# Layer 0 of a four-layer conditioned network: the quantised values are transposed by a DMA, the down projection stands at the step's end, and the y path runs one tile later

## The reference, cut to what matters

```python
def act_quant(x):
    scale = 127.0 / jnp.clip(jnp.max(jnp.abs(x), axis=-1, keepdims=True), 1e-05, None)
    return jnp.clip(jnp.round(x * scale), -128.0, 127.0) / scale
scale = cond @ norm_w.T + 1.0
ms = jnp.mean(x * x, axis=-1, keepdims=True)
h = x * (scale[:, None, :] * jax.lax.rsqrt(ms + EPS))
u = h @ up_w.T                                  # 256 -> 2 x 1024
val, gate = jnp.split(u, 2, axis=-1)
h = val * jax.nn.gelu(gate, approximate=False)
hq = h + jax.lax.stop_gradient(act_quant(h) - h)      # whole numbers -127..127, per token
wq = down_w + jax.lax.stop_gradient(weight_quant(down_w) - down_w)   # -1, 0, 1 times a scale
y = hq @ wq.T                                   # 1024 -> 256
return y + x
```

## Time and profile before

| | |
|---|---|
| median of 3 runs | 845.87 us (844.93 to 846.77) |
| profiled execution | 844.1 us, its span 842.3 us |
| granted clock | 0.99 over the span |
| PE busy | 807.0 us, 96% of the span |
| DVE, POOL, ACT busy | 65%, 49%, 48% |

### The profile page before, as it was taken

One profiled execution on the slowest core, in us unless ns is written; L12 is line 12 of the kernel. 1 busy time (PEld: TensorE's weight loads), 2 busy tenths in 40 slices (PEclk: granted clock), 3 DMA queues, 4 the chain that ended last, 5 costly groups with the idle time before them and its releaser, 6 DMA issues.

```text
span 842.3 us, 20010 instructions
## 1 busy us (share of the span) xinstructions
PE 807.0 (96%) x7116; PEld 645.7 (77%) x7116; DVE 543.9 (65%) x933; ACT 405.1 (48%) x761; POOL 411.2 (49%) x451
## 2 busy tenths in 40 slices
PE   8999999999989999999999999999999999999984
PEld 7878778777868888998898766667667677777862
DVE  4767666666759988898887356545455545444664
ACT  4445544544466778888876322432223232322332
POOL 4444554555568798888886341313131313101555
PEclk9999999999999999999999999999999999999997
DMA  8511011101100000000001267777677677592442
GB/s 259 195 39 38 28 34 37 37 25 38 37 13 2 29 15 3 0 0 0 0 1 30 72 195 234 222 201 219 190 213 197 201 202 192 182 348 101 159 145 100
DMA packets 39940, 89.19 MB, mean 106 GB/s; under 512 B 4816, under 2 KB 14224, under 8 KB 39760
## 3 DMA queue, kind: packets, MB, share of 16 engines
q1 hardware_dynamic: 37296, 84.29, 32.8%
q10 hardware_dynamic: 2592, 4.20, 1.3%
HBM read 67.23 MB, written 21.23 MB: 105 GB/s over the span
## 4 chain that ended last, share of the span: by engine, by line
PE 44%; POOL 14%; issue 7%; ACT 3%; DMA 1%; DVE 1%; POOLq 1%; SPq 1%; ACTq 0%; DVEq 0%
PE bank L1078 20%; PE bank L1092 11%; POOL p_sb L851 4%; PE bank L1112 4%; POOL mlp_in L186 2%; PE bank L382 2%; POOL mlp_in L190 2%; POOL mlp_in L192 1%; PE bank L1611 1%; POOL x_sb L860 1%; PE bank L1623 1%; PE bank L1600 1%; DMA adapter_w<-gen_made 1%; POOL att_in_lo L195 1%; ACT p_sb L1190 1%
## 5 line engine op out<-in xcount | busy, mean ns | idle before, releaser
L1439 DVE TENSOR_TENSOR g<-bank,silu 128x512 f32<-128x512 f32 x64 | 44.2, 690 | 106.3 <-ACT silu L1288 56.5
L623 DVE SCALAR_TENSOR_TENSOR h<-bank,rstd,gelu 128x512 f32<-128x512 f32 x64 | 48.0, 750 | 71.7 <-ACT gelu L508 71.1
L1288 ACT ACTIVATE silu<-bank 128x512 f32<-128x512 f32 x64 | 38.2, 597 | 111.6 <-PE bank L1078 111.6
L1294 ACT ACTIVATE g_hi<-g 128x512 fp32r<-128x512 f32 x64 | 40.4, 632 | 98.3 <-DVE g L1439 96.3
L382 PE MATMUL bank<-up_hi,xs_hi 128*128 128x512 f32 x256 | 85.3, 414 | 1.5 <-POOL xs_lo L319 1.5
L1442 DVE TENSOR_TENSOR g_lo<-g,g_hi 128x512 fp32r<-128x512 f32 x64 | 52.7, 824 | 45.3 <-ACT g_hi L1294 45.3
L1078 PE MATMUL bank<-mlp_in_hi,w_hi 128*128 128x512 f32 x256 | 80.6, 396 | 0.0
L382 PE MATMUL bank<-up_lo,xs_hi 128*128 128x512 f32 x256 | 80.1, 394 | 0.0
L1078 PE MATMUL bank<-mlp_in_lo,w_hi 128*128 128x512 f32 x256 | 79.8, 393 | 0.0
L1078 PE MATMUL bank<-mlp_in_hi,w_lo 128*128 128x512 f32 x256 | 79.7, 392 | 0.0
L851 POOL TENSOR_TENSOR p_sb<-p_sb,rec 128x512 f32<-128x512 f32 x64 | 66.7, 1045 | 26.3 <-DVE rec L1396 26.3
(11 more groups left out here) (196 smaller groups left out, 2019.5 us busy)
## 6 DMA issues: line engine op xcount, KB each, us to landing
gen_hyper<-in_gen_t SPq DMA_DIRECT2D x32, 512.0 KB, 4.8
gen_made<-base_w SPq DMA_DIRECT2D x64, 256.0 KB, 3.9
adapter_w<-gen_made SPq DMA_DIRECT2D x64, 256.0 KB, 3.6
tokens<-in_x_tok SPq DMA_DIRECT2D x32, 128.0 KB, 2.1
w_stage<-in_w_t SPq DMA_DIRECT2D x32, 128.0 KB, 2.1
weight_slot<-adapter_w SPq DMA_DIRECT2D x4, 1024.0 KB, 9.1
w_hi<-adapter_w SPq DMA_DIRECT2D x4, 1024.0 KB, 5.8
w_lo<-adapter_w SPq DMA_DIRECT2D x4, 1024.0 KB, 9.7
```

Source lines behind the costliest of these rows:

```text
L623: nc.vector.scalar_tensor_tensor(out=h[:, k, j * 512:(j + 1) * 512], in0=bank[2 * j][:, :], scalar=rstd0[:, bass.ds(t, 1)], in1=gelu[:, j, ...
L1288: nc.scalar.activation(silu[:, f % 2, :], bank[2 * (f % 2)][:, :], ACT.Silu).then_inc(S["silu_done"], 1)
L1294: nc.scalar.activation(gs[0][:, f % 2, :], g[:, f % 2, :], ACT.Copy).then_inc(S["g_hi_done"], 1)
L1439: nc.vector.tensor_tensor(g[:, f % 2, :], bank[2 * (f % 2) + 1][:, :], silu[:, f % 2, :], ALU.mult).then_inc(S["g_done"], 1)
```

## The change

The transposes of `q` leave PE and the copy of them leaves ACT. SP issues one DMA transpose a tile, SBUF to SBUF, from `q[:, k]` to `qt[:, k]`, as the first thing of its step, ahead of the two loads. PE's step becomes up_chunk 0, up_chunk 1, row_squares, y_transposes, down. `take_y` and `y_transposes` get lag 3, `add_y` and `square` lag 4, `sum_squares`, `row_squares` and `take_row_squares` lag 5. ACT's step becomes take_y, gate 0, square, gate 1, (early_rstd), w1_high, square_tokens. `y` is accumulated in bank 4, and the transposed y and the row sums share bank 7, which brings waits between their users. There is one more step `e36` in the attention's beginning.

```diff
+        def transpose_q(s):
+            if s.live(3):
+                k = s.slot(3, 2)
+                sp.wait_ge(Z["q_done"], s.at(3) + 1)
+                wait(sp, Z["y_ready"], s.at(5) + 1 if s.live(5) else 0)
+                hold(sp, Z["sp_passed"])
+                sp.dma_start_transpose(qt[:, k], q[:, k]).then_inc(qt_loaded[k], 16)
         def body(s):
+            transpose_q(s)
             wait(sp, Z["w1_lo_done"], s.at(3))
             load_stage(s)
             sp.wait_ge(Z["squared_done"], s.at(3))
             load_tokens(s)
...
                 load_x(a, a + 512, "loaded_x")
+            if done == 3:
+                transpose_q(Step(3, 3, N))
         pipeline(sp, N, 0, 4, body, start=4)
+        for t in range(N, N + 3):
+            transpose_q(Step(t, t % 4, N))
...
     def down(pe, s):
-            pe.wait_ge(Z["qt_done"], s.at(2) + 1)
+            pe.wait_ge(qt_loaded[s.slot(2, 2)], 16 * s.turn(2, 2))
...
     def row_squares(pe, s):
-        if s.live(4):
-            pe.wait_ge(Z["sq_sum_done"], s.at(4) + 1)
+        if s.live(5):
+            pe.wait_ge(Z["sq_sum_done"], s.at(5) + 1)
+            wait(pe, Z["ss_done"], s.at(5))
+            pe.wait_ge(Z["x_done"], s.at(3) if s.live(3) else N)
...
-    def q_transposes(pe, s):
...
-            for f in range(FC):
-                last = nc.tensor.transpose(qt_ps[:, f, :], q[:, s.slot(1, 2), f * P:(f + 1) * P], core["ident_bf"][:])
-            last.then_inc(Z["qt_ready"], 1)
...
             up_chunk(pe, s, 0)
-            if not s.first_tile(2):
-                down(pe, s)
             up_chunk(pe, s, 1)
...
             row_squares(pe, s)
             y_transposes(pe, s)
-            q_transposes(pe, s)
+            down(pe, s)
...
-    def take_q(act, s):
...
-            nc.scalar.activation(qt[:, s.slot(2, 2)], qt_ps, ACT.Copy).then_inc(Z["qt_done"], 1)
...
         def body(s):
-            take_q(act, s)
+            take_y(act, s)
+            gate(s, 0)
             square(act, s)
-            gate(s, 0)
-            take_y(act, s)
             if s.last(0):
                 w1_high(s)
             gate(s, 1)
+            if s.last(-3):
+                early_rstd()
...
     def quantise(ve, s):
-            wait(ve, Z["qt_ready"], s.at(2))
+            if s.live(3):
+                ve.wait_ge(qt_loaded[k], 16 * s.turn(3, 2))
...
     def take_row_squares(ve, s):
-        if s.live(4):
+        if s.live(5):
+            ve.wait_ge(Z["ss_ready"], s.at(5) + 1)
+            ve.wait_ge(Z["yt_ready"], s.at(3) + 1 if s.live(3) else N)
...
             values(a2)
-            first["q_transposes"](pe, e32)
             first["row_squares"](pe, e32)
             first["y_transposes"](pe, e32)
+            first["down"](pe, e32)
...
+            first["row_squares"](pe, e34)
+            first["y_transposes"](pe, e34)
             pipeline(pe, NA, 5, 2, attention_body, start=3, stop=NA + 1)
```

More of the change, by code:

```diff
@@ L402, in row_squares, with y_transposes @@
     def row_squares(pe, s):
-        if s.live(4):
-            pe.wait_ge(Z["sq_sum_done"], s.at(4) + 1)
-            if s.first_tile(4):
-                pe.wait_ge(Z["cond_done"], 4)
[L407 to L415, removed]
+        if s.live(5):
+            pe.wait_ge(Z["sq_sum_done"], s.at(5) + 1)
+            wait(pe, Z["ss_done"], s.at(5))
+            pe.wait_ge(Z["x_done"], s.at(3) if s.live(3) else N)
+            nc.tensor.matmul(ss_ps, core["ones"][:], sq_sum[:, s.slot(5, 2), :], start=True, stop=True).then_inc(Z["ss_ready"], 1)
+    def y_transposes(pe, s):
+        if s.live(3):
+            pe.wait_ge(Z["y_done"], s.at(3) + 1)
+            if s.first_tile(3):
+                pe.wait_ge(Z["cond_done"], 4)
+            wait(pe, Z["x_done"], s.at(3))
+            if not s.live(5):
+                wait(pe, Z["ss_done"], s.at(5))
             for d in range(DH):
@@ L451, in body @@
                 nc.tensor.matmul(down_ps, core["ones"][:], wscale[:, 0:1], start=True, stop=True).then_inc(Z["down_total"], 1)
+            row_squares(pe, s)
+            y_transposes(pe, s)
             if s.first_tile(2):
-                down(pe, s)
                 pe.wait_ge(Z["down_step"], 1)
@@ L765, in layers @@
         Z, N0 = first["sems"], T // P
-        e32, e33, e34, e35 = (Step(t, t % 4, N0) for t in range(N0, N0 + 4))
+        e32, e33, e34, e35, e36 = (Step(t, t % 4, N0) for t in range(N0, N0 + 5))
         a1, a2 = (Step(t, t % 2, NA) for t in (1, 2))
@@ L863, in attention_body @@
                 make = s.live(0)
+                if s.first_tile(3):
+                    first["sum_squares"](pool, e35)
                 normalise(s, 2)
@@ L874, in attention_body @@
                     attention_input(nc, pool, core, s.at(0), s.slot(0, 2), 2)
+                if s.first_tile(3):
+                    first["sum_squares"](pool, e36)
                 if s.first_tile(4):
@@ L890, in _ @@
             first["gpsimd"](pool)
+            first["sum_squares"](pool, e32)
             pool.wait_ge(Z["up_done"], 2 * N0)
@@ L895, in _ @@
             attention_input(nc, pool, core, 2, 0, 1)
+            first["sum_squares"](pool, e33)
             first["w1_low"](pool, e32)
-            first["sum_squares"](pool, e32)
-            first["sum_squares"](pool, e33)
             first["w1_low"](pool, e33)
@@ L1057, in attention_body @@
                 keys(s)
+                if s.first_tile(3):
+                    first["row_squares"](pe, e35)
                 weighted_values(s)
@@ L1063, in attention_body @@
                 if s.first_tile(3):
-                    first["row_squares"](pe, e35)
+                    first["row_squares"](pe, e36)
             def hidden_chunk(s, f):
@@ L1124, in _ @@
             keys(a1)
-            first["down"](pe, e32)
             pe.wait_ge(Z["h_done"], 2 * N0)
@@ L1138, in _ @@
             queries(a2)
-            first["row_squares"](pe, e34)
-            pe.wait_ge(Z["x_done"], N0)
+            first["down"](pe, e33)
             transposes(a2, 0)
             transposes(a2, 1)
+            first["row_squares"](pe, e34)
+            first["y_transposes"](pe, e34)
             pipeline(pe, NA, 5, 2, attention_body, start=3, stop=NA + 1)
@@ L1275, in attention_body @@
                 take_keys(s)
+                if s.first_tile(3):
+                    first["square"](act, e35)
                 output_high(s)
@@ L1307, in _ @@
             first["scalar"](act)
-            first["take_q"](act, e32)
             attention_input_high(nc, act, core, 1, 1)
+            first["take_y"](act, e32)
             take_keys(a1)
-            first["take_y"](act, e32)
             take_queries(a1)
@@ L1315, in _ @@
             first["square"](act, e32)
-            first["take_q"](act, e33)
             nc.scalar.preload_act_table_set("natural_log_exp_and_others")
@@ L1320, in _ @@
             attention_input_high(nc, act, core, 2, 0)
-            first["square"](act, e33)
             exponentials(a2, 0)
             exponentials(a2, 1)
+            first["square"](act, e33)
             take_keys(a2)
-            first["square"](act, e34)
             exponentials(a2, 2)
             take_queries(a2)
+            first["take_y"](act, e34)
             exponentials(a2, 3)
+            first["square"](act, e34)
             take_transposed(a2, 0)
@@ L1423, in attention_body @@
                 take_values(s)
+                if s.first_tile(3):
+                    first["take_row_squares"](ve, e34)
+                    first["add_y"](ve, e35)
                 maxima(s, 0)
                 maxima(s, 1)
+                if s.first_tile(3):
+                    first["take_row_squares"](ve, e35)
                 scaled_output(s)
@@ L1431, in attention_body @@
                 if s.first_tile(3):
-                    first["take_row_squares"](ve, e35)
+                    first["take_row_squares"](ve, e36)
             def gated(s, f):
@@ L1488, in _ @@
             maxima(a2, 3)
-            first["take_row_squares"](ve, e34)
             pipeline(ve, NA, 5, 2, attention_body, start=3, stop=NA + 1)
```

78 lines of the change are left out of this document (33 added, 45 removed).

## The result

The changed kernel takes 815.84 us (median of 4 runs, 815.61 to 816.17) against 845.4 beside it (842.67 to 846.77): a ratio of 0.965 with a 95% interval of 0.963 to 0.968, 29.6 us less. The forecast was 825.8 with a range of 817 to 846.

A forecast was written before the change was run, and what follows sets the result against it. Layer 0 was taken as PE-bound with few holes. Transposes 14.4, stalls for y 3.3 and step 28 3.4, less 1.0 at the start, gave 20.1 us: from 845.87 to 825.8, range 817 to 846.

The forecast's parts named there:

- transposes, 24 steps of the loop: Layer 0's loop: q_transposes leave PE, 0.53 us saved in each of 24 steps, all on PE's path.
- waits and holes in the loop: Layer 0's loop: PE's 6 stalls for late y, 3.3 us in all, would go.
- down and y path moved: Layer 0's loop: the new waits over bank 7 would be hidden and cost nothing.
- steps 28 to 31, early_rstd included: Last steps of layer 0: transposes saved at 0.42 us a step, and the 3.4 us stall at step 28 gone.
- start: Steps 0 to 3: tile 4's tokens, queued behind the DMA transpose, make y late for PE; 1.0 us lost.
- behind layer 0: Hand-over to the attention: its start moves with layer 0's end, net within 0.5 us of nothing, counted 0.
- part 3: Layer 0's loop: y path one tile later, so the 3.3 us of PE's stalls for y go.
- X: SP's time from starting the transpose's issue to its next possible load; taken as 2.8 us, lower end 0.4, upper 16.
- the room: Layer 0's loop: 9 us between q's end and the down that needs its transpose, so PE would not wait.
- the circle and its price per step: Two-step loop through SP's token load, ACT and q; harmless up to X 3.9 us, above it the step is (X + 10.2) / 2.
- half rival of blocks in turn: DMA transpose runs its blocks one after another, 1 us or more each, kernel some 925 us; chance 0.10.
- early_rstd: Step 28: placed behind gate 1 on ACT, its 4.5 us are just hidden and PE's stall goes; 3.4 us gained.

The follow-up runs named there:

- e6: Kernel before, transposes still on PE, with only POOL's sum of squares moved one tile later; 837.06 us, ratio 0.990.
- e8: Changed kernel with four plain copies of q to DRAM issued by SP ahead of the transposition; 830.28 us, one run.
- e11: Changed kernel with four plain copies of q to DRAM, SP's two loads put ahead of copies and transposition; 813.59 us, one run.
- e7: Changed kernel with POOL's sum_squares put ahead of the attention's inputs in steps 30 and 31; 815.54 us, ratio 0.965.
- e12: Changed kernel run again with nothing altered, for another trace; 814.5 us, span 812.6.
- e3: Kernel before run again with nothing altered, for a second trace; 845.4 us, span 843.6.
- e15: Kernel before with 60 idle one-column products on PE ahead of its first step; only the part behind layer 0 read, 579.2 us.
- e10: Changed kernel with q transposed by eight DMAs of 128x128 on SP in place of one; 958.2 us, one run.

## Why the prediction was right in direction and short in size

Its sum against the first pair of traces, in us of gain:

| term | forecast | measured | from |
|---|---|---|---|
| transposes, 24 steps of the loop | 12.7 | 12.0 | 7.37 - 6.87 |
| waits and holes in the loop | 3.3 | 8.9 | 7.74 - 7.37 |
| down and y path moved | 0 | 1.4 | 6.87 - 6.81 |
| steps 28 to 31, early_rstd included | 5.1 | 4.1 | the rest of layer 0 |
| start | -1.0 | -2.4 | step 4 at 43.80, not 41.41 |
| behind layer 0 | 0 | 4.4 | 582.6, 578.2 |
| sum | 20.1 | 28.4 | spans: 28.4 |

**The step that failed** is the term of the y path, part 3, with the sentence it stands on: "These long waits of POOL and ACT cost nothing of themselves; what reaches PE is 3.3 us in 6 stalls". The step was 7.06 by (30.97 - 4 x 0.53 - 0.6) / 4 and measured 6.81. The 0.6 a turn was the one stall that the list of waits shows; the order of before really cost 4 x 0.37 = 1.5 a turn, as e6 shows by one moved line. That stall itself is 0.8 when read from start to start (row_squares to y_transposes 117.21 to 118.22 in the kernel before, 0.22 when nothing is late). The rest lay in holes too short for a row of their own, spread over the steps: row_squares took up to 0.33, y_transposes up to 0.28 and q_transposes 0.53, where e6 has 0.22, 0.22 and 0.42. The prediction added such pieces up to 7.67 and took them for work. And "cost nothing of themselves" is the sentence that the experiments turn round: the long waits of POOL and ACT were the circle that set the step. It is also why the DMA alone gave 0.2%: the two gains do not stand side by side as in the sum; with the circle closed the first is worth nothing.

**The transposition.** X was taken as 2.8 and is 1.47, inside the bounds 0.4 to 16, and harmless as forecast; the room, the circle and its price per step held (e8, e11). ACT waits for the tokens and PE does not. The half rival of blocks in turn came near for a change that issues eight DMAs: 925 estimated, 958 measured, with SP's own work and not the circle setting the step, and TensorE's granted clock at 0.86 on average in the loop. "VectorE: DVE Perf Modes", section "The three transpose paths", of the Trainium skill has 1309 ns for 128x128. Here a 128x128 costs SP 1.25 us, close to it, and lands in 2.4; a 128x1024 costs SP the same and lands in 3.1. So the figure must not be multiplied by eight where one DMA carries eight blocks.

**early_rstd.** Forecast 3.4. At step 28 the wait of 3.40 is gone, 0.25 is lost in its place (219.73 to 226.78 is 7.05). Right.

**Steps 30 and 31.** A wait of 1.02 for POOL's sum at 234.34 was not foreseen: the sum stands behind the attention's inputs. e7 shows that little is to be had there.

**The start.** Forecast 1.0 lost by a wait for the tokens; lost 2.4 (43.80 against 41.41), but PE waited for no y. It waited 1.01 for the conditioning weights at 21.15, its granted clock was then 0.66 and 0.50 from 22 to 26 us, and it waited 0.79 for DVE's h at 37.07. The second pair of traces has it the other way round: step 4 at 41.37 in the changed kernel (e12) and 42.32 in the one before (e3). Mostly chance, then, and the term's own reason did not come about.

**Behind layer 0.** Forecast nothing; two pairs of traces give 4.4 and 2.4. It is no effect of the moved work as far as e15, one run, can show. Without it the change would be at 818 to 820, inside the range; with the y term sized right as well, the forecast would have met it. So two things put the result below the range: the y term, 7.0 us short with the moved y path in it, and these microseconds, which nothing in the change earned.

## What to carry to other kernels

An engine busy at 98% can still be paced by a circle of the others: add up its pieces at the length that they have where nothing waits, compare with the step, and look for a round of small waits that comes back to its own start. Then two edits may each give little and much together, or one moved line (here POOL's sum of squares, 0.37 us a step) may be the better half of a large change. Count DMA transpositions by issues, not by blocks, and see what SP issues behind them.

## What the runs showed of the hardware

- A DMA transposition costs SP 1.23 to 1.27 us per issue in the loop, for 128x128 (e10) as for 128x1024 of bf16, where a plain load of a tile mostly costs 0.33 to 0.43. It lands in 2.4 and 3.1 us (medians). With four plain copies a step beside it, the issue takes 1.5 us and the landing 3.9 (medians of e8 and e11).
- While the input is loaded at some 386 GB/s, the first transposition holds SP for 2.27 us and the traffic falls by half. SP's issues, then the windows from 26 to 30 us, changed kernel:

```profile
23.34 2.27 SPq L271 DMA_TRANSPOSE qt<-q  x1
26.82 1.87 SPq L250 DMA_DIRECT2D x_sb<-in_x_t  x3
26.00:28.00 2.00, 2.00 (x15) 1.53 (x13) 0.00 (x0) 1.07 (x3) 0.96 (x2) 0.99 1.82 182
28.00:30.00 2.00, 2.00 (x11) 1.65 (x11) 1.76 (x6) 0.81 (x3) 1.92 (x3) 1.00 0.68 175
```

  The kernel before moves 386 and 387 GB/s in the same stretches, and in the changed kernel it is 389 again from 30 to 32 us. From 26 to 28 the DMA engines are busy (1.82) and move little; from 28 to 30 they are partly idle (0.68), as the next loads of x went out only at 26.82. How much of the loss is the transposition itself and how much the late loads, these traces do not tell. That first transposition took 6.8 us to land, the slowest of the 32.
- PE can stand 1.7 to 2.9 us within a group of products with no semaphore behind it, at places that moved when idle instructions were put ahead of them; in all ten cases a packet of an instruction queue starts within 0.9 us of the hole's start.
- A product of one column with 128x128 4-byte weights took 0.36 to 0.40 us in the shifted runs (120 in 47.6 us, 60 in 22.3 and 21.6, with the granted clock at 0.50 from 20 us on while they ran), so such fillers are not free.
